# A step's three projections in another order: q, v, k in place of v, q, k

## The reference

```
Q = split_heads(x @ Wq.T + bq)      # the same for K, V
cQ = Q + split_heads(tokens @ Wq.T + bq)
cK = K + split_heads(tokens @ Wk.T + bk)
scores = einsum('bhqd,bhkd->bhqk', cQ, cK) / sqrt(32)
out = einsum('bhqk,bhkd->bhqd', softmax(scores), V)
return x + out                      # all float32
```

## Time and profile before

| | |
|---|---|
| median of 3 runs | 644.05 us |
| the profiled execution | 645.23 us |
| its span on the core | 643.4 us |
| TensorE (PE) busy | 636.5 us, 99% |
| VectorE (DVE) busy | 543.8 us, 85% |
| GpSimd (POOL) busy | 488.1 us, 76% |
| ScalarE (ACT) busy | 388.3 us, 60% |
| granted TensorE clock | 1.0 of full speed over the span |

### The profile page before, as it was taken

One profiled execution on the slowest core, in us unless ns is written; L12 is line 12 of the kernel. 1 busy time (PEld: TensorE's weight loads), 2 busy tenths in 40 slices (PEclk: granted clock), 3 DMA queues, 4 the chain that ended last, 5 costly groups with the idle time before them and its releaser, 6 DMA issues.

```text
span 643.4 us, 10063 instructions
## 1 busy us (share of the span) xinstructions
PE 636.5 (99%) x3528; PEld 438.0 (68%) x3528; DVE 543.8 (85%) x818; ACT 388.3 (60%) x684; POOL 488.1 (76%) x204
## 2 busy tenths in 40 slices
PE   8999999999999999999999999999999999999997
PEld 6777677666677666677666677666776666776542
DVE  6886888888888888888888888888888888998887
ACT  6465666565566565566565666566666555564773
POOL 6438877778877779877779777779777778666991
PEclk9999999999999999999999999999999999999999
DMA  7944334555334555334555334555344565424501
GB/s 245 270 108 118 105 102 97 146 151 148 99 104 100 147 150 137 101 105 107 149 149 132 104 101 115 150 151 129 102 103 116 149 164 136 116 71 120 144 24 61
DMA packets 48243, 80.83 MB, mean 126 GB/s; under 512 B 9545, under 2 KB 9801, under 8 KB 48073
## 3 DMA queue, kind: packets, MB, share of 16 engines
q1 hardware_dynamic: 47837, 80.04, 47.6%
q10 hardware_dynamic: 356, 0.16, 0.1%
HBM read 19.95 MB, written 8.39 MB: 44 GB/s over the span
## 4 chain that ended last, share of the span: by engine, by line
PE 95%; DVE 2%; issue 1%; DMA 1%; ACT 1%; SPq 0%; POOLq 0%; DVEq 0%; ACTq 0%
PE bank L352 27%; PE bank L445 18%; PE bank L427 18%; PE bank L465 17%; PE bank L400 14%; DMA Pt<-xT 1%; DVE bank L744 1%; ACT Pt L640 1%; DVE part_sums L769 0%; DVE rr L793 0%; DVE ends L814 0%; PE bank L473 0%; DVE rr L782 0%; DVE bank L800 0%; PE bank L377 0%
## 5 line engine op out<-in xcount | busy, mean ns | idle before, releaser
L640 ACT ACTIVATE Pt<-bank 128x512 f32<-128x512 f32 x512 | 299.0, 600 | 207.3 <-PE bank L445 136.0
L744 DVE TENSOR_REDUCE mf<-bank 128x1 f32<-128x512 f32 x496 | 330.7, 684 | 61.8 <-PE bank L427 59.7
L953 POOL TENSOR_TENSOR A<-A,Pt 128x2048 f32<-128x2048 f32 x59 | 271.6, 4603 | 4.6
L427 PE MATMUL bank<-Ks,Qs 128*128 128x512 f32 x496 | 195.9, 396 | 0.2
L445 PE MATMUL bank<-Qs,Ks 128*128 128x512 f32 x496 | 195.4, 400 | 0.1
L953 POOL TENSOR_TENSOR A<-Pt 128x2048 f32<-128x2048 f32 x30 | 138.3, 4608 | 9.3 <-ACT Pt L640 5.0
L445 PEld LDWEIGHTS bank<-Qs,Ks 128*128 128x128 f32 x496 | 92.6, 188 | 48.7 <-ACT Pt L640 26.1
L465 PE MATMUL bank<-Pt,V 128*32 128x512 f32 x1024 | 118.9, 596 | 0.0
L427 PEld LDWEIGHTS bank<-Ks,Qs 128*128 128x128 f32 x496 | 93.0, 187 | 28.4 <-DVE mf L744 6.0
L923 POOL TENSOR_TENSOR Xl<-xr,Xh 128x512 fp32r<-128x512 f32 x28 | 36.3, 1297 | 98.9 <-ACT Xh L601 98.9
L352 PE MATMUL bank<-Xh,Wh 128*128 128x512 f32 x256 | 100.2, 392 | 0.9 <-ACT Xh L587 0.8
(11 more groups left out here) (74 smaller groups left out, 394.0 us busy)
## 6 DMA issues: line engine op xcount, KB each, us to landing
Qs<-hi SPq DMA_DIRECT2D x60, 256.0 KB
Ks<-hi SPq DMA_DIRECT2D x60, 256.0 KB, 3.8
Qs<-lo SPq DMA_DIRECT2D x30, 256.0 KB
Ks<-lo SPq DMA_DIRECT2D x30, 256.0 KB, 3.8
xr<-xT SPq DMA_DIRECT2D x28, 256.0 KB, 2.7
res<-xT SPq DMA_DIRECT2D x28, 256.0 KB, 2.9
outT<-ot SPq DMA_DIRECT2D x28, 256.0 KB, 3.6
Qs<-mt SPq DMA_DIRECT2D x122, 4.0 KB
```

Source lines behind the costliest of these rows:

```text
L427: e.matmul(MXB[u % 2][:, :], q[:, j, qc * P:(qc + 1) * P], k[:, j, :], start=True, stop=True).then_inc(t_mx, 1)
L640: e.activation(exponentials(g)[:, kc, j, :], st_bank(u)[:, :], ACT.Exp, scale=SCALE).then_inc(a_e, 1)
L744: e.reduce_max(to[:, 4 * j + qc:4 * j + qc + 1], MXB[u % 2][:, :], AXX).then_inc(v_mx, 1)
L953: e.tensor_tensor(sums, ex[:, 0, :, :] if kc == 1 else sums, ex[:, kc, :, :], ALU.add).then_inc(p_a, 1)
```

## The change

Three constants and one string differ. In steps 0 to 24 the list of projections is q, v, k. The value copy moves from slot 4 to slot 10, the query's high copy from slot 10 to slot 7, its low copy from slot 11 to slot 8, and the high part of x from slot 5 to slot 4. The key's copies keep their slots.

```diff
-V_AT, X_COND_AT, X_AT, Q_HI_AT, K_HI_AT = 4, 2, 5, 10, 16
-Q_LO_AT, K_LO_AT = 11, 17
+V_AT, X_COND_AT, X_AT, Q_HI_AT, K_HI_AT = 10, 2, 4, 7, 16
+Q_LO_AT, K_LO_AT = 8, 17
...
-                kinds = "vqk" if t < G - EARLY else "qkv"
+                kinds = "qvk" if t < G - EARLY else "qkv"
```

## The result

The changed kernel took 655.96 us (median of 4 runs, 654.27 to 657.26) against 644.25 us; the ratio is 1.0176, interval 1.0157 to 1.0195. It is slower, as forecast; 652.9 was predicted, in a range of 650.3 to 656.8. Its profiled execution took 657.26 us with a span of 655.5.

A forecast was written before the change was run, and what follows sets the result against it. TensorE's queue was taken to bound steps 1 to 24. A 0.44 us stop less 0.07 returned gave 0.37 a step, 24 x 0.37 = 8.9 us, so 644.05 + 8.9 = 652.9 us, range 650.3 to 656.8.

The forecast's parts named there:

- What bounds the kernel: Steps 1 to 24: TensorE's queue alone sets the 19.39 us pace; any wait put into it lengthens the step one for one.
- The order and its takes: TensorE's bank takes: slots 0 and 5 cost nothing; slot 9, the key, now waits for the query's low pass.
- When the low pass ends: VectorE slot 8: the low pass ends late, so TensorE stops 0.44 us a step at the key's first matmul.
- What comes back: Slots 12 to 1: with the low pass out of slot 11, 0.07 of 0.09 us a step returns.
- the sum: Steps 1 to 24: stop minus relief, 0.44 - 0.07 = 0.37 us a step, 8.9 us in all; step 0 unchanged.
- rival C: Key's first matmul: a larger stop, up to 0.66 us a step, 655 to 660 us; chance 0.11.
- part 2: The term on when VectorE's low pass of the query ends: a 0.44 us stop, bounds 0.31 to 0.66 a step.
- B: Rival: the ring hides the copy, stop of 0.04 to 0.14 us a step, 643 to 645.3 us; chance 0.05.
- Other moves: Value copy leaving slot 4, x one slot earlier, query's DMA, turned maxima: no effect on the step's length.
- A: Rival: the wait is covered, only slots 14 to 1 give back 0.09 us a step, 641.9 us; chance 0.04.
- What I said the profile would show: L352's load waits for L734, some 0.4 us each, about 10 us; L427, L400 and L601 waits shrink; step 19.76 us.

The follow-up runs named there:

- e7: Kernel before plus one TensorE wait in steps 1 to 24: the key's first matmul also waits for slot 9's row maxima; 665.14 us against 644.06, ratio 1.0333.
- e6: Kernel before, old order, with the query's high copy in slot 9 and low pass in slot 10 instead of 10 and 11; 642.92 us against 644.06, ratio 0.9982.
- e8: The changed kernel run again with nothing altered; 655.15 us against 644.06 for the kernel before, ratio 1.0171.
- e9: Changed kernel with the high part of x back in slot 5 instead of 4; 654.74 us, ratio 1.0156 to the kernel before.
- e5: Kernel before, old order, with only the high part of x moved from slot 5 to slot 4; 653.98 us against 644.06, ratio 1.0152.
- e1: Changed kernel with the query's high copy in slot 6 and low pass in slot 7 instead of 7 and 8; 642.87 us against 644.16 before, ratio 0.9977.
- e4: Changed kernel with VectorE's two key-sum passes in slots 3 and 5 instead of 4 and 6; 653.78 us against 644.16 before, ratio 1.0150.
- e3: Changed kernel with the query's low pass in slot 9 instead of 8; 684.02 us in a single run.
- e2: Changed kernel with the key's first matmul moved from slot 9 to slot 10 in TensorE's order; 643.93 us against 644.16 before, ratio 0.9993.

## Why the prediction was right, point by point

**What bounds the kernel**: right. TensorE's queue alone sets the pace in steps 1 to 24, and a wait put into it counts one for one (e7).

**The order and its takes**: right. Slots 0 and 5 got no wait; slot 9 did, in 24 steps, at the key's first matmul.

**When the low pass ends**: the place and the chain of events were right, the size of the stop a little small. I had the low pass 13.47 to 14.21 us into the step and measured 13.44 to 14.17 (327.45 less the step's start at 314.01); the stop was 0.46 against 0.44. The two distances behind the pass came out otherwise than in my row: the load starts 0.05 us behind the end of the pass, as there (0.052 to 0.054 in all 24 steps), but the matmul is recorded with its load and not 0.08 behind it, and the next matmul follows 0.33 us later, 0.10 more than a distance. The strict reading of the rule in the Trainium skill, "VectorE: DVE Perf Modes", section "The DRAIN you can't avoid", is not borne out: the low pass again starts 0.08 us before the recorded end of the pass in front.

**What comes back**: I took 0.07. Slots 13 to 15 gave back 0.05, in the changed kernel as in e6. The waits for row maxima that I expected to go went for the most part (table of waits, before and after):

```profile
PEld bank L427 <- DVE mf L744: 6.5, 32, 0.3
PEld bank L427 <- DVE mf L744: 1.9, 9, 0.3
```

The place was right, the size 0.02 too large. In slots 15 to 1 loads of L427 still start 0.05 to 0.06 us behind the end of a row maxima pass, and matmuls there up to 0.236 us apart (step 14 of the changed kernel).

**What the sum missed**: a step grew by 0.446 us, against 0.37. Slot 9 is 0.48 longer, slots 10 and 11 together 0.04 longer, slots 13 to 15 0.05 shorter, slots 0 to 4 0.02 shorter (0.01 in e8). The 0.04 was no term of mine: behind the stop, ten matmuls start 0.230 us apart (328.57 to 330.87) instead of 0.2267. So the mis-sized term is the stop, 0.44 for what is 0.52 with its tail, and 24 x 0.446 = 10.7 us instead of 8.9. With it 644.05 + 10.7 = 654.8, and e8 measured 655.15; the four times behind 655.96 lie 3 us apart.

**What the time alone would have said.** 655.96 lies above the forecast's own range, 651.3 to 654.5, and inside that of rival C, 655 to 660. The stated range holds it only because it took in half of C. It is the profile that tells the forecast from C. Two figures of the prediction do not come out of its own terms: by the release times of part 2 the new copy is 0.44 us too late for B, not 0.31, and 0.1 us a step below 652.9 is 650.5, not 650.3. Neither changes the forecast.

**Other moves**: right, within the new order (e9). In the old order the x part alone costs 9.3 us (e5), which my text did not say: it is free only because the value copy leaves slot 4.

**The rivals.** A's relief is real (0.06 us a step in e6), but the wait was not covered. B fell: the ring hides the copy only where the copy's place lets it (e1). The rule of the Trainium skill in "Perfetto Trace Analysis", section "Optimizing Tensor Performance", holds in e1, where the low pass ends 0.07 us before the load, and not in the changed kernel: rotation alone was not enough with its two banks. C had the sign of the error right, the stop being larger than my row gave, but not the cause: no low pass of the query waited for ScalarE in steps 1 to 24, the matmul did not start a full 0.22 behind its load, and the relief did come.

**What I said the profile would show**: the wait of L352's load for L734 is there, 24 times; its sum is 14.7 us, not about 10, since the loads' idle time is longer than the stop. ScalarE's wait for L400 fell from 27 times to 2, both ahead of the main loop. GpSimd's wait for L601 fell from 98.9 to 70.6 us and moved no step.

## What to carry to other kernels

Where a ring has few banks, moving a producer also moves the deadline of the copy that frees its bank: list for each take which copy it waits for, and compare the end of that copy, by its place in its own engine's queue, with the start of the load that needs it. A slot of 1.13 us decided here between 0.2% faster (e1) and 1.7% slower. Price a stop by the distance between starts of matmuls, not by the table of waits or the shares of the chain, and add a little for the matmuls behind it.

## What the runs showed of the hardware that was not expected

After a stop TensorE does not return to its pace at once: with the same tiles and no further recorded wait, matmuls start 0.230 us apart for two slots instead of 0.2267. Slots 10 and 11 together are 0.03 to 0.04 us longer in the changed kernel, e4, e7, e8 and e9, and 0.02 in e3. In e2, where a load waited 0.16 us and no matmul stood still to speak of, the two slots with their ten matmuls take 2.307 us instead of 2.267, as much as behind the full stop. In e1 and e6, where no load of a projection waited, they have their old length. So a load that waited is common to all the cases. Why it should matter is open; no run here takes it apart.
